# A three-stage network on one core: the first control of a data-dependent loop is worked out from token 0 during the scan

## The reference, cut to what matters

```python
xs, z = split(tn @ W_in)                     # tn: normed tokens
delta, Bv, Cv = xs @ W_delta, xs @ W_B, xs @ W_C
# per image, from state 0:
state = exp(delta_i * A) * state + (delta_i (x) Bv_i) * xs_i
y_i   = state @ Cv_i                         # y: 64 channels
t = t + (y * silu(z)) @ W_out
...
def step(h, p):                              # 33 times, h = layer_norm(t)
    op = argmax(h[0, 0, :19])                # token 0 of image 0
    y = attention(h, p, op); h = where(p.am[op], y, h)
    z = relu(h @ w1[op] + b1[op]) @ w2[op] + b2[op]
    h = where(p.fm[op], z, h)
```

## Time and profile before

| what | value |
|---|---|
| median of 3 runs | 319.19 us (317.14 to 551.79) |
| the profiled execution, its own time | 318.29 us |
| span from first to last instruction in it | 316.3 us |
| mean granted TensorE clock | 0.873 |
| busy share PE / DVE / ACT / POOL | 80% / 76% / 68% / 54% |

### The profile page before, as it was taken

How to read it: one execution, slowest core, us unless ns; L and a number is a source line. 1 busy time by engine, 2 the same in 40 slices (tenths; PEclk the granted TensorE clock), 3 DMA queues, 4 the chain that set the end, 5 groups by cost and what they waited for, 6 DMA issues and landing times. The chain is left out here.

```text
span 316.3 us, 6004 instructions
## 1 busy us (share of the span) xinstructions
PE 253.5 (80%) x2422; PEld 148.7 (47%) x2422; DVE 239.9 (76%) x183; ACT 215.3 (68%) x298; POOL 170.8 (54%) x105
## 2 busy tenths in 40 slices
PE   8798999999796444496689568968699897799983
PEld 3255777777352100053375336634476764335730
DVE  0339999991359799999999999999999983124461
ACT  1047777776357799989999999999996441152350
POOL 1160000000093799999999999999998971000000
PEclk9999999999999755569766995597758999999998
DMA  3500000000003000000000000000000000000001
GB/s 108 191 0 2 2 0 2 2 2 2 0 9 93 0 0 0 1 2 2 1 0 2 2 2 0 0 2 2 2 2 2 2 0 2 13 10 10 0 0 33
DMA packets 2505, 4.00 MB, mean 13 GB/s; under 512 B 687, under 2 KB 1712, under 8 KB 2480
## 3 DMA queue, kind: packets, MB, share of 16 engines
q1 hardware_dynamic: 2216, 3.38, 3.6%
q10 hardware_dynamic: 264, 0.26, 0.3%
HBM read 2.59 MB, written 0.26 MB: 9 GB/s over the span
## 5 line engine op out<-in xcount | busy, mean ns | idle before, releaser
L778 DVE TENSOR_TENSOR_SCAN pool<-ps,pool 128x1024 f32<-128x1024 f32 x63 | 143.9, 2290 | 5.3 <-POOL pool L453 2.8
L453 POOL TENSOR_TENSOR pool<-pool 128x1024 f32<-128x1024 f32 x58 | 135.0, 2351 | 7.1 <-ACT pool L571 6.0
L1090 PE MATMUL ps<-pool,picks 96*128 96x512 bf16 x120 | 50.1, 512 | 40.7 <-DVE pool L778 40.7
L581 ACT ACTIVATE ps<-ps,a_cols 128x1020 f32<-128x1020 f32 x64 | 69.4, 1085 | 8.2 <-DVE pool L755 6.3
L571 ACT ACTIVATE pool<-ps 128x1024 f32<-128x1024 f32 x58 | 59.2, 1021 | 6.9 <-PE ps L1090 3.0
L518 ACT ACTIVATE pool<-ps 128x1024 f32<-128x1024 f32 x36 | 34.9, 1022 | 13.2 <-PE ps L986 13.2
L274 DVE TENSOR_TENSOR pool<-pool 128x2048 f32<-128x2048 f32 x18 | 40.1, 2284 | 0.9 <-ACT pool L499 0.9
L1112 PE MATMUL ps<-pool 128*32 128x112 f32 x1024 | 39.6, 293 | 0.0
L1112 PEld LDWEIGHTS ps<-pool 128*32 128x32 f32 x1024 | 30.8, 124 | 17.9 <-issue 17.9
L416 POOL MEMSET pool<- 128x4096 f32 x1 | 3.5, 3512 | 66.0 <-DVE tn L717 66.0
L1090 PEld LDWEIGHTS ps<-pool,picks 96*128 96x128 bf16 x120 | 8.2, 109 | 61.9 <-DVE pool L778 59.9
(11 more groups left out here) (166 smaller groups left out, 239.1 us busy)
## 6 DMA issues: line engine op xcount, KB each, us to landing
pool<-ssm_w_dram SPq DMA_DIRECT2D x1, 896.0 KB, 5.3
pool<-pool SPq DMA_DIRECT2D x12, 64.0 KB, 2.0
pool<-offset_w_dram SPq DMA_DIRECT2D x1, 576.0 KB, 6.7
cst<-const_dram SPq DMA_DIRECT2D x1, 426.0 KB, 3.2
pool<-conv_w_dram SPq DMA_DIRECT2D x1, 144.0 KB, 3.2
pool<-w_up_dram SPq DMA_DIRECT2D x2, 64.5 KB
pool<-x_dram SPq DMA_DIRECT2D x1, 128.0 KB
pool<-x_dram ACTq DMA_DIRECT2D x1, 128.0 KB
```

What stands on the lines that cost most here:

```text
L453: pool_e.tensor_tensor(dbx[e % 3], bx, delta_wide[n % 2], ALU.mult).then_inc(pool_dbx_ready, 1)
L581: act.activation(decay[:, :, 1:HW], decay[:, :, 1:HW], ACT.Exp, scale=a_cols[:, PER * g + j:PER * g + j + 1]).then_inc(da_ready, 1)
L778: dve.tensor_tensor_scan(state[e % RING], slot(e), dbx[e % 3], 0.0, ALU.mult, ALU.add)\
L1090: ins = pe.matmul(slot(e)[:, column_half(c)], picks[:, j * 128:(j + 1) * 128], stack[0:96, g * SEQ + c * BANK:g * SEQ + (c + 1) * BANK], s ...
```

## The change

Token 0's row is worked out during the scan from its own small products: one gate column (PE ahead of the delta projection, Silu on ACT), its delta and its B C x sum (PE at turn 4, bank 0), their product (ACT at turn 5, DVE at turn 7), the output projection plus `t1` (PE at turn 9). DVE then runs the first control's instructions one or two at a time behind scans 11 to 17 (`early_control`), with `ctl_ready` behind scan 17. `wup` and `wdn` move from the big tile to a tile `shared`, over `row0_picks`, whose last reader is the fourth spread; SP waits for that, and then loads the first weights as soon as the control is there. After layer norm 1 no row, no control and no 14 keep_warms stand ahead of the loop; ten keep_warms move from the loop's start to its end.

```diff
@@ -63,7 +63,10 @@
         picks = sb("picks", [96, PER * 128], bf16)
-        row0_picks = sb("row0_picks", [128, GROUPS * 128], bf16)
+        shared = sb("shared", [128, GROUPS * 64])
+        row0_picks = shared[:, :].bitcast(bf16)
+        wup, wdn = shared[:, 0:HID + 1], shared[:, HID + 8:HID + 8 + C + 1]
+        first = sb("first", [128, 3])
         zero_bf = sb("zero_bf", [128, BANK], bf16)
@@ -148,8 +151,6 @@
-        wup = region("ffn", HID + 4)[:, 0:HID + 1]
-        wdn = region("ffn", C + 4)[:, 0:C + 1]
         qs, ks, vt, vo = (region("ffn", TOK) for _ in range(4))
@@ -241,6 +242,8 @@
             sem, ["gated_ready", "mix_done", "last_prod_ready", "table_input"])
+        first_gate_in, first_gate_ready, first_done, first_scaled, first_ready = map(
+            sem, ["first_gate_in", "first_gate_ready", "first_done", "first_scaled", "first_ready"])
         eps_set, firsts_ready = sem("eps_set"), sem("firsts_ready")
@@ -337,6 +340,7 @@
             layer, op = regs[0], regs[1]
+            sp.wait_ge(delta_spread, GROUPS)
             sp.wait_ge(ctl_ready, 1)
@@ -382,7 +386,7 @@
-            pool_e.tensor_copy(row0_picks[:, :].rearrange("p (k d) -> p k d", k=GROUPS * HALVES),
+            pool_e.tensor_copy(row0_picks.rearrange("p (k d) -> p k d", k=GROUPS * HALVES),
                                ident.rearrange("p (k j) -> p k j", j=PER)[:, :, 0].unsqueeze(2)
@@ -535,6 +539,8 @@
             act.activation(gate, bank(6, 2), ACT.Silu).then_inc(gate_ready, 1)
+            act.wait_ge(first_gate_in, 1)
+            act.activation(first[:, 0:1], bank(4)[:, 0:1], ACT.Silu).then_inc(first_gate_ready, 1)
             for c in range(2):
@@ -581,6 +587,9 @@
                 act.activation(decay[:, :, 0], zero_bf[:, 0:PAIRS], ACT.Copy).then_inc(da_ready, 1)
+                if e == 5:
+                    act.wait_ge(first_done, 1)
+                    act.activation(first[:, 1:2], bank(0)[:, 1:2], ACT.Copy, scale=first[:, 0:1]).then_inc(first_scaled, 1)
                 if e >= BATCH + 2 and on_pool(e):
@@ -770,6 +779,53 @@
+            regs = control_registers(dve, "dve")
+            steps_done, attns, ffns = counters(dve, "dve")
+            op_reg = dve.alloc_register("dve_chosen")
+            def candidates():
+                dve.load([op_reg], idx[0:1, 0:1])
+                op = dve.snap(op_reg, min_val=0, max_val=OPS - 1)
+                v = cand[:, :].rearrange("p (s l) -> p s l", s=3)
+                return v, dve.scalar_tensor_tensor(
+                    v, stepno[:, 0:LAYERS].unsqueeze(1).broadcast_to([1, 3, LAYERS]), cur[:, 0:1],
+                    tab[:, bass.ds(op * (3 * LAYERS), 3 * LAYERS)].rearrange("p (s l) -> p s l", s=3),
+                    ALU.is_gt, ALU.mult)
+            def early_control(e):
+                row = bank(0)[0:1, 8:8 + OPS]
+                if e == 7:
+                    dve.wait_ge(first_scaled, 1)
+                    dve.tensor_tensor(first[:, 2:3], bank(0)[:, 0:1], first[:, 1:2], ALU.mult).then_inc(first_ready, 1)
+                elif e == 11:
+                    dve.wait_ge(row_done, 1)
+                    dve.max(top[:, :], row).then_inc(ctl_step, 1)
+                elif e == 12:
+                    dve.wait_ge(ctl_step, 1)
+                    dve.max_index(idx[:, :], top[:, :], row).then_inc(ctl_step, 1)
+                elif e == 13:
+                    settle()
+                    dve.wait_ge(ctl_step, 2)
+                    candidates()[1].then_inc(ctl_step, 1)
+                elif e == 14:
+                    dve.wait_ge(ctl_step, 3)
+                    dve.tensor_reduce(best[:, 0:3], cand[:, :].rearrange("p (s l) -> p s l", s=3), AX.X, ALU.max)\
+                       .then_inc(ctl_step, 1)
+                elif e == 15:
+                    dve.wait_ge(ctl_step, 4)
+                    dve.tensor_scalar(cur[:, :], best[:, 0:1], -1.0, float(LAYERS), ALU.mult, ALU.add)\
+                       .then_inc(ctl_step, 1)
+                    dve.tensor_scalar(ctl[:, 2:4], best[:, 1:3], best[:, 0:1], None, ALU.is_equal).then_inc(ctl_step, 1)
+                elif e == 16:
+                    dve.tensor_copy(ctl[:, 1:2], idx[:, 0:1]).then_inc(ctl_words, 1)
+                    dve.wait_ge(ctl_step, 5)
+                    dve.tensor_copy(ctl[:, 0:1], cur[:, :]).then_inc(ctl_words, 1)
+                elif e == 17:
+                    dve.wait_ge(ctl_words, 2)
+                    dve.wait_ge(ctl_step, 6)
+                    dve.sem_inc(ctl_ready, 1)
             added(0)
@@ -779,6 +835,7 @@
                     gate_batch(e // BATCH - 2)
+                early_control(e)
@@ -805,10 +862,6 @@
-            regs = control_registers(dve, "dve")
-            steps_done, attns, ffns = counters(dve, "dve")
-            op_reg = dve.alloc_register("dve_chosen")
             def next_step(n):
@@ -818,12 +871,8 @@
                 hold(dve, ctl_step, c + 2)
-                dve.load([op_reg], idx[0:1, 0:1])
-                op = dve.snap(op_reg, min_val=0, max_val=OPS - 1)
-                v = cand[:, :].rearrange("p (s l) -> p s l", s=3)
-                dve.scalar_tensor_tensor(v, stepno[:, 0:LAYERS].unsqueeze(1).broadcast_to([1, 3, LAYERS]), cur[:, 0:1],
-                                         tab[:, bass.ds(op * (3 * LAYERS), 3 * LAYERS)]
-                                         .rearrange("p (s l) -> p s l", s=3), ALU.is_gt, ALU.mult).then_inc(ctl_step, 1)
+                v, ins = candidates()
+                ins.then_inc(ctl_step, 1)
                 dve.wait_ge(ctl_step, c + 3)
@@ -844,8 +893,7 @@
             dve.sem_inc(ctl_read, 1)
-            next_step(0)
-            publish(0)
+            dve.load(regs, ctl[0:1, 0:4])
             with dve.While(lambda: dve.snap(regs[0]) < LAYERS):
@@ -1052,9 +1100,11 @@
             pe.wait_ge(xs_ready, 1)
+            pe.matmul(bank(4)[:, 0:1], wt["w_gate"][:, 0:128], tn[:, 0:1], start=True, stop=True).then_inc(first_gate_in, 1)
             project(2, wt["w_delta"], delta_done)
...
+            pe.wait_ge(first_gate_ready, 1)
             project(4, wt["w_c"], c_done)
@@ -1140,10 +1190,25 @@
+            def first_token_early(e):
+                if e == 4:
+                    pe.wait_ge(bx_ready, 1)
+                    pe.matmul(bank(0)[:, 0:1], wt["w_delta"], xs[:, 0:1], start=True, stop=True)
+                    pe.matmul(bank(0)[:, 1:2], cn[0:DI, 0:1].broadcast_to([DI, 128]), bx[0:DI, 0:1], start=True, stop=True)\
+                      .then_inc(first_done, 1)
+                elif e == 9:
+                    pe.wait_ge(first_ready, 1)
+                    row = bank(0)[0:1, 8:8 + C]
+                    pe.matmul(row, first[:, 2:3], wt["w_out"][:, 0:C], start=True, stop=False)
+                    pe.matmul(row, t1[0:C, 0:1], ident[0:C, 0:C], start=False, stop=True).then_inc(row_done, 1)
             for e in range(DI):
                 spread_delta(e)
+                first_token_early(e)
                 if e == BATCH + 2:
                     pe.wait_ge(c_placed_ready, 4)
+                    pe.wait_ge(ctl_step, 2)
                 if e >= BATCH + 2:
@@ -1203,13 +1268,10 @@
-            first_token(1)
-            keep_warm(14)
             pe.wait_ge(ctl_ready, 1)
...
                 pe.reg_add(steps_done, steps_done, 1)
-                keep_warm(10)
                 with pe.If(pe.snap(regs[2]) > 0):
@@ -1319,7 +1381,7 @@
                     first_token(1 + pe.snap(attns) + pe.snap(ffns))
-                keep_warm(6)
+                keep_warm(16)
                 hold(pe, ctl_ready, pe.snap(steps_done) + 1)
```

## The result

| | before | changed |
|---|---|---|
| median | 318.53 us (20 runs) | 316.73 us (20 runs) |
| ratio, 95% interval | | 0.9936 [0.9912, 0.996] |
| profiled execution, its own time | 318.29 us | 315.61 us |
| span | 316.3 us | 313.7 us |

A forecast was written before the change was run, and what follows sets the result against it. DVE and POOL were taken as practically full during the scan; after it, 7.71 us of control and weight load bound the path. Terms: -7.25 + 0.25 + 0.6 + 0.2 = -6.2, from 318.29 to 312.1 us, range 311.2 to 313.0.

The forecast's parts named there:

- So I take half of the busy time: DVE's control instructions at e = 11 to 16 delay scans by half their busy time: 0.2 us, plus 0.6 swallowed later.
- My own sign of being wrong: In the scan: the forecast is wrong if scans drift by more than 2 us.
- the scan paying in full: Rival: register load exposed, stalls swallow nothing, control chain's 2.4 us moves into the scan; 3.55 added, 314.6 us; chance 0.18.
- Absorption: DVE's waits for POOL at scans 17 to 19, 0.8 us in all, swallow 0.6 us of delays of scans 14 to 16: +0.
- The wait at e = 9: PE's wait for DVE's product ahead of the spread of row 10 delays it: +0.6 us (0.3 to 1.0).
- Max and index: DVE's first two control instructions, at e = 11 and 12 in the scan: +0.2 us.
- Ahead of the scan: PE's extra fp32 matmul before the delta projection shifts the first scan: +0.25 us, bounds 0 and 0.5.
- PE's start: After the scan, PE's first up matmul starts at 269.1 instead of 276.37, h complete at 268.66: about 7.25 us gained.
- The clock: PE's clock at the feed-forward start, granted at 1.00 before: no loss priced for the 24 removed keep_warms.
- The taken branch: Rival: PE's branch over the attention code stalls like a 3.02 us DMA fetch instead of 0.354; 314.8 us; chance 0.04.
- The second step: Feed-forward's following step through PE keeps its length, starting 10.4 us after the first: nothing gained, nothing lost.

The follow-up runs named there:

- 3: Changed kernel with the early control's table step reading a fixed table slice, without its register load; 316.7 us, ratio 0.9942.
- 7: Changed kernel plus only four keep_warms behind the transposes of the second layer norm; 315.22 us, ratio 0.9878.
- 8: Changed kernel with SP waiting for h before it loads the first control and weights; 322.37 us, ratio 1.013.
- 4: Changed kernel with token 0's row made by PE at turn 10, behind the spread of row 10, instead of turn 9; 315.96 us, ratio 0.9934.
- 1: Changed kernel with the table step reading one input, the step numbers, from PSUM; 313.11 us, ratio 0.982.
- 5: Changed kernel with a table step input from PSUM, flags written one by one, and token 0's row behind spread 10; 313.08 us, ratio 0.9837.
- 6: Kernel of 5 plus four keep_warms ahead of the first control's load; 312.34 us, ratio 0.9795.
- 11: Kernel of 6 plus eight keep_warms ahead of spread 3 and two behind each of spreads 4 to 15; 315.58 us, ratio 0.9928.
- 12: Kernel of 6 plus only eight keep_warms ahead of spread 3; 310.48 us, ratio 0.9719.
- 13: Kernel of 6 plus 32 one-column matmuls of zeros behind spreads 4 to 15; 315.21 us, ratio 0.9874.
- experiment 10: Kernel before, with the table step on scratch data behind scans 24, 36, 30 and 50, the latter two after four one-element instructions; 320.58 us, ratio 1.0066.
- experiment 9: Kernel before, with one tiny DVE instruction on scratch data behind each of six single scans; 320.58 us, ratio 1.0067.

## Why the prediction was wrong, step by step

**The step that failed** is the pricing of DVE's additions inside the scan, "So I take half of the busy time": the table step at 0.15 and the scalars at 0.18 us, from durations read where POOL is idle and from a gate product that reads PSUM. In the scan these two waited for POOL's product: scan 14 came 2.27 us late and scan 16 2.13, 4.4 us where I had 0.6 to be swallowed. My own sign of being wrong, a drift of the scans by more than 2 us, came true with 3.9. The price was in no row of the piece of trace I had taken it from, and I had read POOL and DVE as two full engines without asking whether they share anything. The Trainium skill says they do ("SBUF — State Buffer", section "SBUF: two separate sides"): a DVE instruction in a mode that uses two ports, or one with two SBUF inputs beside a GpSimd instruction that reads SBUF (POOL's product does), and the GpSimd instruction exclude each other for the whole instruction. The runs agree, with 0.1 to 2.3 us by arrival. Where one of the table step's inputs is in PSUM (0.28), and where an instruction with a single input has one element (0.12 to 0.19), there is no wait. Why two elements wait and one doesn't I have only as rows. The Trainium skill ("VectorE: DVE Perf Modes", section "What auto-detection actually checks") gives as condition of a two-port mode a single source and a destination in SBUF whose outermost non-unit dimensions are both even or equal. Two elements meet it; one element has no such dimension, which would fit, but no run here shows the mode.

**The rival that I priced next to it**, the scan paying in full (314.6), had the right sign and the wrong mechanism: no load was exposed, and the scan lost more (5.2 us in the changed kernel's profile) than the control chain's 2.4 and the 0.9 at e = 9.

**Absorption was right.** "Delays of scans 14 to 16 are swallowed at scans 17 to 19": 0.27 + 0.31 + 0.40 = 0.98 us came back there. But 0.98 of 4.4, not of 0.6. And about 1.4 more was lost later, at single scans between 20 and 47. From scan 3 to scan 62 it is 143.0 us before and 148.2 in the changed kernel, and so (148.1 to 148.3) in 3, 7 and 8, which have both waits too, but 147.2 in 4; in the kernels without either wait (1, 5, 6, 11 to 13) it is 143.0 to 143.6. So this loss goes with the two waits; what sets single late scans I leave open.

**The wait at e = 9**: forecast 0.6, measured 0.41 at scan 10. Max and index: forecast 0.2, measured 0.05. Both oversized, by 0.3 together.

**Ahead of the scan**: forecast 0.25. The layer norm's product started at 85.70 instead of 86.33, before anything that was changed, and scan 0 at 99.72 instead of 100.20. That leaves 0.15.

**PE's start**: forecast 0.44 us behind h, measured 0.8 in every profile of the changed code but 8 (late weights), 11 and 13 (long branch). The start was forecast 0.36 too early. One part is that the control load began 0.29 us after the transposes were released (271.31 against 271.02), not 0.13. Half of the 0.36 is the length of the load: I had put its 0.52 down to three engines that load at once, but PE's first load takes 0.52 in every profile and its later ones 0.34, alone or not.

**The clock**: "I price no loss of clock for the removed 24". Wrong: experiments 6 and 7 put it at about 0.7 and 1.5 us between medians, and it is 0.6 us in the changed kernel's own profile. The row I used was of a stretch with 5.37 us of filler in it, the very thing that is removed.

**The taken branch**: the rival at 0.04 (2.65 us dearer) didn't come true in the changed kernel, but it does with 32 matmuls more ahead of the branch, at 3.3 and 3.6 us. The Trainium skill's rule ("Runtime: NRT & Kernel Launch", section "Instruction fetch mechanics") fits these rows; that a fetch is what takes the time no run here shows. Before the change the wait for weights, until 276.19, would have covered most of such a branch.

**The second step** kept its length: 278.73 + 5.50 = 284.23 against a start at 273.22 is 11.0 us, 10.4 of before and 0.6 of clock.

In sum, profile to profile: -6.9 at the hand-over, +0.6 clock, +0.3 between scan 62 and h (the granted clock was 0.90 there, 1.00 before), +3.9 in the scan (5.2 lost, less 1.3 since scan 3 came at 7.33 instead of 8.60), -0.5 ahead: -2.6. The 1.3 is no merit of the change: scan 3 came anywhere from 7.3 to 8.6 in the profiles of kernels that do the same there. Nor is the 0.63 by which the layer norm came earlier. Both are luck of the profiled pair; the profiles are 2.7 us apart, the medians 1.8.

## What to carry to other kernels

A duration holds for the neighbours it was measured with: before a small DVE instruction is moved beside a busy POOL, look whether it reads two SBUF tensors, or copies or scales more than one element from SBUF to SBUF; one input in PSUM, or, with a single input, one element at a time, made it cheap here. When a wait on DMA is taken off the path, list what it had covered, here the registers, the branch and the clock, and price each uncovered. And look at the branch's own row after every edit ahead of it.

## What the runs showed of the hardware that I had not expected

- The same instruction took 0.30 or 2.38 us as it came 0.09 us before or after the start of a POOL product (experiment 10); at 0.04 us before a start it already waited for the whole product (2.50 us, experiment 9).
- PE's taken branch over the attention code took 0.35 us in thirteen kernels and 3.3 to 3.6 in the two that had 32 more matmuls ahead of it (11 and 13).
- The spread of row 3, behind a 2.4 us wait of PE, took from 1.47 us (granted clock 1.00) to 2.74 (0.50), and scan 3 came up to 1.3 us earlier or later by it. With eight matmuls of zeros in the wait it took 1.47 in both profiles (11, 12), but also in three of the ten of the changed code without them, so that they hold the clock is not shown. The kernel with them and a short branch (12) has the lowest median of the study.
